# Moving a broadcast multiply of quantised weights from GpSimd to VectorE in a fused attention and mixture-of-experts block

## The reference

```
h   = smooth_quant_linear(layernorm(x), W1)      # W1 512x512 (fside)
a   = silu(h[:, :256]) * h[:, 256:]
x   = x + tanh(g_xattn) * smooth_quant_linear(a, W2)   # W2 512x256 (ctx)
x   = x + tanh(g_ffn) * moe(layernorm(x))        # 16 experts, top 2, and a shared expert

def smooth_quant_linear(x, w):
    s = sqrt(max(|x| over tokens) / max(|w| over rows))   # one value for each channel
    xs, ws = x / s, w * s
    x_scale, w_scale = max |xs| of a token / 127, max |ws| of a row / 127
    return round(xs / x_scale) @ round(ws / w_scale).T * x_scale * w_scale.T
```

## Time and profile before

| what | value |
|---|---|
| median of 3 runs | 684.85 us (684.42 to 687.08) |
| the profiled execution | 685.71 us, its span 684.0 us |
| busy PE, DVE, ACT, POOL | 520.7, 423.1, 291.2, 154.4 us |
| mean granted clock of TensorE in the profiled execution | 0.888 |

### The profile page before, as it was taken

The page is one execution under the profiler, slowest core; times in us unless marked ns, Lnnn a source line. Parts: engine busy times, 40 slices in busy tenths (PEclk is TensorE's granted clock), DMA queues, the critical chain, the costliest instruction groups (busy, mean ns, idle before and its releaser), DMA issues.

```text
span 684.0 us, 8403 instructions
## 1 busy us (share of the span) xinstructions
PE 520.7 (76%) x3080; PEld 424.5 (62%) x3080; DVE 423.1 (62%) x633; ACT 291.2 (43%) x402; POOL 154.4 (23%) x138
## 2 busy tenths in 40 slices
PE   0235433899898998999789999999999999995000
PEld 0222312578566875577557779999999999994000
DVE  5835799576577757642657676666666665661354
ACT  2076445416732556234233145556655665552000
POOL 2400384013000310010000143132123212100773
PEclk9855555899999999999999999999999999999555
DMA  7800011100110001300000056777677668701786
GB/s 282 310 29 33 1 31 61 62 1 31 52 73 0 0 31 54 133 2 0 40 23 1 4 177 202 257 261 233 196 271 260 211 219 261 240 31 64 236 269 229
DMA packets 42199, 83.32 MB, mean 122 GB/s; under 512 B 4080, under 2 KB 22512, under 8 KB 41152
## 3 DMA queue, kind: packets, MB, share of 16 engines
q1 hardware_dynamic: 37056, 66.23, 28.3%
q0 software_dynamic: 5120, 16.78, 8.1%
HBM read 66.23 MB, written 16.78 MB: 121 GB/s over the span
## 4 chain that ended last, share of the span: by engine, by line
PE 63%; DVE 17%; ACT 7%; POOL 5%; issue 5%; DMA 2%; POOLq 0%; DVEq 0%; SPq 0%
PE ps_gu L1099 12%; PE ps_gu L1101 12%; PE ps_gu L1100 12%; PE ps_d L1099 5%; PE ps_d L1101 5%; PE ps_d L1100 5%; POOL got L484 4%; PE ps_a L1138 2%; PE ps_a L1333 2%; DVE y L746 1%; PE ps_a L1145 1%; DVE bn_b L735 1%; DMA tg<-in_g_ffn 1%; DVE sh_hid L820 1%; PE ps_a L1199 1%
## 5 line engine op out<-in xcount | busy, mean ns | idle before, releaser
L1099 PE MATMUL ps_gu<-ex_xhi,w_hi 128*128 128x256 f32 (+1 forms) x384 | 110.3, 287 | 1.1 <-DVE ex_xlo L1039 1.1
L1100 PE MATMUL ps_gu<-ex_xlo,w_hi 128*128 128x256 f32 (+1 forms) x384 | 108.0, 281 | 0.0
L1101 PE MATMUL ps_gu<-ex_xhi,w_lo 128*128 128x256 f32 (+1 forms) x384 | 107.9, 281 | 0.0
L1099 PE MATMUL ps_gu<-xt_hi,sw_hi 128*128 128x512 f32 x176 | 72.1, 410 | 7.5 <-DVE sh_hid L820 7.2
L1099 PEld LDWEIGHTS ps_gu<-ex_xhi,w_hi 128*128 128x128 f32 (+1 forms) x384 | 69.6, 181 | 6.1 <-issue 3.9
L1100 PEld LDWEIGHTS ps_gu<-ex_xlo,w_hi 128*128 128x128 f32 (+1 forms) x384 | 69.6, 181 | 0.7
L1101 PEld LDWEIGHTS ps_gu<-ex_xhi,w_lo 128*128 128x128 f32 (+1 forms) x384 | 69.8, 182 | 0.0
L1100 PE MATMUL ps_gu<-xt_lo,sw_hi 128*128 128x512 f32 x176 | 69.0, 392 | 0.0
L1101 PE MATMUL ps_gu<-xt_hi,sw_lo 128*128 128x512 f32 x176 | 68.9, 391 | 0.0
L453 POOL DMA_INDIRECT xg<-x2n_scratch,idx_col x32 | 52.1, 1629 | 18.0 <-POOL idx_col L449 13.1
L1025 DVE TENSOR_TENSOR w_lo<-raw_gu,w_hi 128x1408 fp32r<-128x1408 f32 x32 | 51.6, 1616 | 0.0
(11 more groups left out here) (234 smaller groups left out, 1125.4 us busy)
## 6 DMA issues: line engine op xcount, KB each, us to landing
raw_gu<-in_L_ffn_w_gate SPq DMA_DIRECT2D x16, 704.0 KB, 4.4
raw_gu<-in_L_ffn_w_up SPq DMA_DIRECT2D x16, 704.0 KB, 5.9
raw_d<-in_L_ffn_w_down SPq DMA_DIRECT2D x16, 512.0 KB, 7.2
expert_out_scratch<-eo SPq DMA_DIRECT2D x16, 512.0 KB, 7.4
w<-in_fside_BxS2xS SPq DMA_DIRECT2D x4, 1024.0 KB, 5.4
x2n_scratch<-y SPq DMA_DIRECT2D x4, 1024.0 KB, 3.9
out<-x SPq DMA_DIRECT2D x8, 512.0 KB, 4.2
x<-in_x SPq DMA_DIRECT2D x1, 3072.0 KB, 17.0
```

Source lines behind the costliest of these rows:

```text
L1099: pe.matmul(dst, a_hi, b_hi, start=start, stop=False)
L1100: pe.matmul(dst, a_hi, b_lo, start=False, stop=False)
L1101: return pe.matmul(dst, a_lo, b_hi, start=False, stop=stop)
```

## The change

VectorE multiplies `w1` and `w2` by the smoothing row straight from PSUM, in `first_activations` and `second_activations`, ahead of the multiply of the activations. ScalarE's copies `row_s_a` and `row_s_b`, the semaphore between them and GpSimd, and GpSimd's `smooth_weights` are gone. `A_S` is now freed by VectorE's multiply.

```diff
--- before.py
+++ after.py
@@ GpSimd
-            def smooth_weights(layer, b, w, row, width):
-
-                pool.tensor_tensor(w[:], w[:], row[:].unsqueeze(1).broadcast_to((P, J, width)),
-                                   ALU.mult).then_inc(ws_done[layer], 1)
-
...
                 if b is not None:
                     root(LB, b, C2)
-                    pool.wait_ge(row_copied, b + 1)
-                    smooth_weights(LB, b, w2, row_s_b, I2)
                 if a is not None:
                     root(LA, a, C)
-                    pool.wait_ge(free[LA], unit(LA, a, A_S))
-                    smooth_weights(LA, a, w1, row_s_a, D)
@@ ScalarE
                 sh_chunk(1)
                 if b is not None:
-                    act.wait_ge(full[LB], unit(LB, b, B_S))
-                    act.activation(row_s_b[:], bank(LB)[:, 0:I2], ACT.Copy).then_inc(row_copied, 1)
                     quantise(b, gated, small[LB]["x_inv"], ar, x_steps[LB], x_scaled[LB], qx_done[LB])
                 sh_chunk(2)
-                if a is not None:
-                    copy_row(LA, a, A_S, row_s_a)
@@ VectorE
             def first_activations(a, wide):
 
+                dve.wait_ge(full[LA], unit(LA, a, A_S))
+                dve.tensor_tensor(w1[:], w1[:], bank(LA).unsqueeze(1).broadcast_to((P, J, D)), ALU.mult).then_inc(free[LA], 1)
                 dve.wait_ge(free[LA], unit(LA, a, A_S))
+                dve.sem_inc(ws_done[LA], 1)
                 dve.wait_ge(full[LA], unit(LA, a, A_RS))
                 dve.tensor_tensor(xn[:], xn[:], bank(LA, 1, wide).unsqueeze(1).broadcast_to((P, J, D)),
                                   ALU.mult).then_inc(free[LA], 1)
...
             def second_activations(b):
-                dve.wait_ge(row_copied, b + 1)
+                dve.wait_ge(full[LB], unit(LB, b, B_S))
+                dve.tensor_tensor(w2[:], w2[:], bank(LB)[:, 0:I2].unsqueeze(1).broadcast_to((P, J, I2)),
+                                  ALU.mult).then_inc(ws_done[LB], 1)
                 dve.tensor_tensor(gated[:], gated[:], bank(LB)[:, I2:2 * I2].unsqueeze(1).broadcast_to((P, J, I2)),
                                   ALU.mult).then_inc(free[LB], 1)
```

## The result

The changed kernel took 701.86 us (699.9 to 705.47, 4 runs), and the kernel before, beside it, 685.97 us (684.42 to 688.39, 4 runs). The ratio is 1.024, 95% interval 1.021 to 1.027. The ratios are not those of the medians, which lie 15.9 us (1.023) and 14.7 us (1.021) apart. The change makes the kernel slower.

A forecast was written before the change was run, and what follows sets the result against it. The prediction took TensorE's waits to bound the loop and VectorE's dependent steps the first two iterations. Terms 2.3+5.0+6.1 = +13.4 us on the 684.85 us median gave 698.3 us, range 691 to 700.

The forecast's parts named there:

- First iteration, +2.3: First iteration: VectorE's new product of `w1` delays the multiply of `xn` and everything behind it, +2.3 us.
- Second iteration, +5.0: Second iteration: GpSimd's split starts earlier, holding `w_step_b` and `smooth_a`; `x_step_a` and `w_step_a` become short, +5.0 us.
- Loop, +3.04 each: Two loop iterations: TensorE stalls 1.06 us for `ar` and 1.98 us for `w1`'s product freeing `A_S`, +3.04 us each.
- the 2.66 us wait: Loop: TensorE's wait before transposing `w1`'s integers, ended by ScalarE's `q_x`; forecast to move along unchanged, at 2.66 us.
- rival C: Loop: stalls are paid from TensorE's 2.66 us wait, 0.38 us per iteration; 686.9 or 692.9 us, chance 0.05.
- Last iteration, 0: Last iteration: only `w2`'s product is added, and `ar` still ends before TensorE wants it, 0 us.
- A: Second iteration: VectorE wins the 0.11 us race for `w_step_b`, only `smooth_a` waits; 692.2 us, chance 0.26.
- B: Second iteration: split starts over 0.4 us later, neither `w_step_b` nor `smooth_a` is held; 689.2 us, chance 0.05.
- D: Second iteration: something more is held, for instance `smooth_a` missing its gap, 2 to 3 us more; 701 us, chance 0.06.
- the errors of my terms: 691 to 700: Whole kernel: the forecast range, 691 to 700 us, said to take in A and the errors of the terms.
- The sum of +13.4: Whole kernel: 2.3 first, 5.0 second and 6.1 us loop iterations added, +13.4 us, giving 698.3 us.

The follow-up runs named there:

- E3: The changed kernel, with both of GpSimd's splits in the second iteration waiting for the steps of `w1`: 693.15 us, ratio 1.0107 to the kernel before.
- E10: The changed kernel, with GpSimd's splits in the second iteration waiting for the steps of `w2`, starting 0.6 us later: 690.36 us, ratio 1.0069 to before.
- E9: The changed kernel again, unedited, in five runs with a third trace (the second comparison): 700.31 us, ratio 1.0226 to the kernel before.
- E1: The kernel before, with only the product of `w2` moved to VectorE, `w1` staying with GpSimd: 690.34 us, ratio 1.0081.
- E2: The kernel before, with only the product of `w1` moved to VectorE, `w2` staying with GpSimd: 696.7 us, ratio 1.0173.
- E5: The kernel before, with GpSimd's three splits of the second iteration placed where VectorE should ask for nothing they hold: 674.94 us, ratio 0.9831.
- E6: The changed kernel with the same placing of GpSimd's splits as E5: 684.81 us, ratio 0.9978 to the kernel before.

## Why the prediction was wrong: its mechanisms held, its size was short

*First iteration, +2.3.* Right: the product of `xn` moved by 2.29, the start of the last product there by 2.50.

*Second iteration, +5.0.* Right in each link: the split first by 0.11 us, `w_step_b` and `smooth_a` held one split each, `x_step_a` and `w_step_a` free again, 5.07 measured. The causal claim was tested by E3 and E10, which move nothing but the split. Over the first two stages the three traces of the changed kernel have 139.9, 140.0 and 140.6 us, and the two of before 133.0 and 131.5; the means differ by 8.0, where the terms gave 7.3. The kernel before alone spreads by 1.5 there, so the 0.7 is not settled.

*Loop, +3.04 each.* Right: from the loop stage's start to the row of 1/s it is 30.84 us here and 30.86 in E9, and 27.82 before, 3.02 and 3.04 more. The stage is 3.1 to 3.2 longer. E1 and E2 give its two parts, 1.1 and 2.0 (as waits of TensorE 1.1 and 1.76, the second 0.2 shorter than forecast). That the two stalls cost what they last, and aren't paid back by the 2.66 us wait, is seen in that wait's unchanged length: rival C fell.

*Last iteration, 0.* Not shown wrong: 68.2 us in two traces, 67.8 and 69.5 before; here the clock alone moves it by more.

*Rivals.* A (only `smooth_a` held) was seen in no trace. B did not happen by itself, and happens with a split 0.6 us later (E10). D, something more held, did not happen in the changed kernel beyond the hold of `y` that before has too; it did in E3, E5 and E6, with the sum.

**The step that failed** is the sum and its range, "the errors of my terms: 691 to 700": its terms were a little short, and TensorE's clock had been put at nothing without a reason. The sum of +13.4 was short of the +15.9 measured (14.7 between the medians of the second comparison). The traces give what can be traced: 8.0 in the first two stages (forecast 7.3), 3.15 in each loop iteration at an undisturbed clock (forecast 3.04), at most 0.4 in the last (forecast 0), together at most 14.7. So 1.3 us were missing in the terms, and the second comparison shows no more than that. The other 1.2 us of the first comparison go with the share of long executions in it, two of four, where seven of all ten lie between 699.1 and 700.9. The base had been taken 1.1 us too low as well (684.85, later 685.97). In the one long execution with a trace the half clock added 1.7 us in the loop and about 3.6 in the last iteration, 5.3 in all; that the other two were long for the same reason is likely, and not shown. I had read the granted clock of 0.98 in the loop as a constant, and given the clock no term and no width. With those 5.3 us the upper end would have been near 705, an estimate from this one trace.

**Still open:** whether the change makes such stretches more frequent. The fall behind the 1.76 us wait came in 1 of 14 loop iterations that have this wait (seven traces), and the long low stretch of the last iteration in 2 of 8 traces with `w2`'s product on VectorE (the changed kernel's and E3's), against none of 4 without it. That is too few to tell, and no run was made to tell it.

## What to carry to other kernels

Before a reader of a PSUM bank is moved to an engine that reads later, look at what TensorE has queued behind that bank's next use: here relieving ScalarE of a 0.58 us copy, and GpSimd of two products, cost TensorE 3 us in each iteration. When an engine is relieved, ask what it starts earlier: a long GpSimd instruction moved under VectorE's small dependent steps cost more than the product itself, and placing three such instructions where VectorE has no step that they hold made the kernel before 1.7% faster. Read the duration of tiny instructions (0.17 us that became 6) and not only the waits, and give a forecast some width for the clock where short TensorE waits are added.

## What the runs showed of the hardware

- VectorE's 128x4 TENSOR_SCALARs were held by a running GpSimd instruction for up to 6.03 us, in place of 0.17, and four of 128x512 took 7.79 us in place of 1.91. So was a VectorE TENSOR_TENSOR with both inputs in SBUF (3.00 and 3.48 for 2.29), and that held GpSimd in turn (14.31 for 12.19). Products with one input in PSUM, a reduce (2.29 us) and RECIPROCAL (0.18) ran at their usual length under a split (E10). The Trainium skill, "SBUF — State Buffer", section "Who interferes with whom", gives this rule: a product contends when both inputs lie in SBUF, a reduce never does, and the one that issues first has the ports for its whole instruction. The trace agrees.
- A held VectorE instruction gets in between two GpSimd instructions that follow each other without a gap. Starts 0.10 to 0.11 us apart in the records told the order in all five traces that had this race.
- The same wait of 1.76 us was followed by TensorE's 1.2 GHz level in one execution and not in another, and the same wait of 3.1 us by a short or a long low stretch. The spread was 5.6 us of 700 for one kernel. The Trainium skill, "TensorE: Matmul & The Clock Gate", section "Part 1: The HAM clock gate (the "warmup" mystery)", says of a kernel's start that the ramp to the high level varies from run to run, and holds its penalty for under 1% of a typical span. The low stretches here lie in the middle of the kernel, and cost 5.3 us of 701.6, 0.8%, in one execution, which is a third of the change's own effect.
